# A gated graph network on one Trainium2 core: the first node tile's tanh stays in PSUM for its difference, its final sum goes to GpSimd, its low words are formed behind the loop

## The reference, cut to what matters

```python
def _gate(h, q, Wg, bg, Wq, bq):
    B, L, F = q.shape                      # 8, 64, 768
    h3 = h.reshape(B, N, F)                # N = 32 nodes for each of 8 graphs
    hg = jnp.einsum('bnf,gf->bng', h3, Wg[:, :F])
    qg = jnp.einsum('blf,gf->blg', q, Wg[:, F:]) + bg
    attn = jax.nn.sigmoid(hg[:, :, None, :] + qg[:, None, :, :])
    qi = jnp.einsum('bnlf,blf->bnf', attn, q)
    alpha = jax.nn.sigmoid(jnp.einsum('bnf,gf->bng', h3, Wq[:, :F]) + jnp.einsum('bnf,gf->bng', qi, Wq[:, F:]) + bq)
    hn = alpha * jnp.tanh(qi) + (1.0 - alpha) * h3
    return hn.reshape(B * N, F)

h = jax.nn.relu(_rgcn(x, W_rel1, W_root1, b1, src, dst, edge_type))
h = _gate(h, query_embs, Wg, bg, Wq, bq)
h = jax.nn.relu(_rgcn(h, W_rel2, W_root2, b2, src, dst, edge_type))
h = _gate(h, query_embs, Wg, bg, Wq, bq)
```

## Time and profile before

| what | us |
|---|---|
| median of 3 runs (lowest to highest) | 878.64 (878.55 to 879.24) |
| the profiled execution | 879.18 |
| its span in the profile | 877.4 |

### The profile page before, as it was taken

The page is one execution under the profiler, slowest core; times in us unless marked ns, Lnnn a source line. Parts: engine busy times, 40 slices in busy tenths (PEclk is TensorE's granted clock), DMA queues, the critical chain, the costliest instruction groups (busy, mean ns, idle before and its releaser), DMA issues.

```text
span 877.4 us, 10143 instructions
## 1 busy us (share of the span) xinstructions
PE 803.3 (92%) x4034; PEld 632.5 (72%) x4034; DVE 604.2 (69%) x671; ACT 388.4 (44%) x448; POOL 502.6 (57%) x214
## 2 busy tenths in 40 slices
PE   8999999999788999988997879999999998987987
PEld 3569976775455798666655459987997897864674
DVE  8955149999997622988999968534853888254451
ACT  1124366777663333766765524432342342241521
POOL 0346629999884472899998917661873478000000
PEclk9999999999999999999999989999999999979999
DMA  9036516254332452440533237633652653600000
GB/s 368 2 87 237 160 54 183 61 151 137 108 108 72 164 169 102 133 106 1 204 112 105 72 120 279 212 109 134 226 180 72 247 189 105 237 14 1 1 1 36
DMA packets 24262, 110.98 MB, mean 126 GB/s; under 512 B 3604, under 2 KB 5908, under 8 KB 23832
## 3 DMA queue, kind: packets, MB, share of 16 engines
q1 hardware_dynamic: 23096, 104.24, 36.3%
q10 hardware_dynamic: 1120, 6.10, 1.8%
HBM read 100.63 MB, written 0.79 MB: 116 GB/s over the span
## 4 chain that ended last, share of the span: by engine, by line
PE 61%; DVE 21%; POOL 12%; ACT 4%; issue 2%; DMA 0%; ACTq 0%; DVEq 0%
PE ps L958 22%; DVE prod L1679 12%; PE ps L906 11%; PE ps L943 6%; POOL prod L544 6%; POOL w_lo L532 4%; PE ps L1335 3%; DVE qi_t L1697 3%; PE ps L1195 2%; PE ps L1017 2%; POOL prod L547 2%; PE ps L1038 2%; PE ps L1148 2%; PE ps L1394 2%; PE ps L1320 1%
## 5 line engine op out<-in xcount | busy, mean ns | idle before, releaser
L532 POOL TENSOR_TENSOR w_lo<-w_raw,w_hi 128x1536 fp32r<-128x1536 f32 x54 | 201.5, 3742 | 148.6 <-ACT w_hi L598 148.5
L544 POOL TENSOR_TENSOR prod<-prod 128x1024 f32<-128x1024 f32 x94 | 223.5, 2400 | 49.1 <-DVE prod L1679 48.7
L705 ACT ACTIVATE prod<-ps 128x1024 f32<-128x1024 f32 x192 | 187.1, 1024 | 78.4 <-PE ps L1148 60.5
L1679 DVE TENSOR_TENSOR prod<-prod,ps 128x2048 f32<-128x2048 f32 x96 | 217.6, 2278 | 5.0 <-ACT prod L705 4.0
L1148 PE MATMUL ps<-sel_pair,h_and_q 128*128 128x512 f32 x384 | 129.7, 450 | 24.6 <-ACT prod L705 24.3
L906 PE MATMUL ps<-w_raw,h_t 128*128 128x384 f32 x408 | 141.7, 494 | 0.0
L598 ACT ACTIVATE w_hi<-w_raw 128x1536 fp32r<-128x1536 f32 x54 | 80.3, 1488 | 136.7 <-PE ps L958 92.9
L958 PE MATMUL ps<-w_hi,yt_hi 128*128 128x384 f32 x432 | 111.6, 339 | 8.1 <-POOL w_lo L532 8.1
L906 PEld LDWEIGHTS ps<-w_raw,h_t 128*128 128x128 f32 x408 | 78.7, 194 | 46.6 <-issue 2.6
L1148 PEld LDWEIGHTS ps<-sel_pair,h_and_q 128*128 128x128 f32 x384 | 67.2, 191 | 60.6 <-ACT prod L705 40.4
L958 PE MATMUL ps<-w_lo,yt_hi 128*128 128x384 f32 x432 | 110.4, 336 | 0.0
(11 more groups left out here) (189 smaller groups left out, 1001.8 us busy)
## 6 DMA issues: line engine op xcount, KB each, us to landing
w_raw<-weights SPq DMA_DIRECT2D x105, 768.0 KB, 4.4
wa_in<-weights SPq DMA_DIRECT2D x6, 768.0 KB, 5.8
w_gat<-weights SPq DMA_DIRECT2D x6, 768.0 KB, 8.0
w_query<-weights SPq DMA_DIRECT2D x3, 768.0 KB, 11.2
h_and_q<-stage_hi SPq DMA_DIRECT2D x24, 96.0 KB, 2.1
h_and_q<-stage_lo SPq DMA_DIRECT2D x24, 96.0 KB, 2.2
a_vec<-gat_vectors ACTq DMA_DIRECT2D x1, 2048.0 KB, 8.2
q_t<-queries ACTq DMA_DIRECT2D x1, 1536.0 KB, 10.6
```

Of the source, the lines that this page charges most:

```text
L532: pool.tensor_tensor(Wl[:, j, :], raw_slab(U, 0, j), Wh[:, j, :], ALU.subtract).then_inc(w_lo_ready, 1)
L544: pool.tensor_tensor(v[:, :, 0:32], v[:, :, 0:32], v[:, :, 32:64], ALU.add).then_inc(folded_once, 1)
L705: act.activation(slot_view(s)[:, :, 32 * u:32 * u + 32], args.rearrange("p b (n l) -> p (b n) l", l=LH), ACT.Sigmoid).then_inc(sigmoid_rea ...
L1679: TT(slot_view(s), slot_view(s), ps[:, 6, o:o + L].unsqueeze(1).broadcast_to([P, NB, L]), ALU.mult).then_inc(products_ready, 1)
```

## The change

The tanh of the first tile stays in PSUM bank 7, written over its own input. `gate_diff` is cut into two parts of 512 and 256 columns that read it there, at steps 29 and 32, and TensorE's next use of the bank waits for the difference, not for the tanh. `gate_add` leaves VectorE and stands in GpSimd's queue behind the fold of step 34. `h_lo` of the first tile leaves steps 38 and 43 and stands behind the loop, between `last_diff` and `last_half`.

```diff
 # GpSimd
+            def gate_add(i):
+                pool.wait_ge(alpha_diff_ready, 3 * i + 1)
+                if i == 0:
+                    pool.tensor_tensor(H[:, 0, :], H[:, 0, :], tq[:], ALU.add).then_inc(h_ready[0], 1)
+                else:
+                    pool.wait_ge(state_added, 1)
+                    pool.tensor_tensor(X[:, 0, :], X[:, 0, :], tq[:], ALU.add).then_inc(gate_x_ready, 1)
...
                 for s in range(STEPS - 1):
                     fold(i, s)
+                    if s == 34:
+                        gate_add(i)
                     if i == 1 and s == 38:
                         rstd(1, 0)
 # ScalarE
                 def gate_tanh(part):
                     act.wait_ge(qi_turned, 4 * i + (part + 1))
-                    c0, c1 = ((0, 512), (512, F))[part]
-                    act.activation(tq[:, c0:c1], ps[:, 7, 0:c1 - c0], ACT.Tanh).then_inc(tanh_ready, 1)
+                    n = (512, F - 512)[part]
+                    act.activation(ps[:, 7, 0:n], ps[:, 7, 0:n], ACT.Tanh).then_inc(tanh_ready, 1)
 # TensorE, bank7_free
                     if kind == "q":
-                        pe.wait_ge(tanh_ready, 4 * i + (m + 1))
+                        pe.wait_ge(diff_ready, 4 * i + (m + 1))
 # VectorE
-                def gate_diff():
-                    dve.wait_ge(tanh_ready, 4 * i + 2)
-                    TT(tq[:], tq[:], H[:, 0, :], ALU.subtract).then_inc(diff_ready, 1)
+                def gate_diff(part):
+                    c0, c1 = ((0, 512), (512, F))[part]
+                    dve.wait_ge(tanh_ready, 4 * i + part + 1)
+                    TT(tq[:, c0:c1], ps[:, 7, 0:c1 - c0], H[:, 0, c0:c1], ALU.subtract).then_inc(diff_ready, 1)
                 def gate_scale():
-                    dve.wait_ge(diff_ready, 3 * i + 1)
+                    dve.wait_ge(diff_ready, 4 * i + 2)
                     dve.wait_ge(alpha_ready, 3 * i + 1)
                     TT(tq[:], tq[:], alpha[:], ALU.mult).then_inc(alpha_diff_ready, 1)
-                def gate_add():
-                    dve.wait_ge(alpha_diff_ready, 3 * i + 1)
-                    if i == 0:
-                        TT(H[:, 0, :], H[:, 0, :], tq[:], ALU.add).then_inc(h_ready[0], 1)
-                    else:
-                        dve.wait_ge(state_added, 1)
-                        TT(X[:, 0, :], X[:, 0, :], tq[:], ALU.add).then_inc(gate_x_ready, 1)
...
                     if h == 0:
-                        dve.wait_ge(diff_ready, 3 * i + 3)
+                        dve.wait_ge(diff_ready, 4 * i + 4)
...
-                    if s == 33:
-                        gate_diff()
+                    if s in (29, 32):
+                        gate_diff((s - 29) // 3)
                     if s == 34:
                         gate_scale()
-                    if s == 35:
-                        gate_add()
-                    if i == 0 and s == 38:
-                        h_lo(1, 0)
                     if i == 1 and s == 36:
                         dve.wait_ge(gate_x_ready, 1)
                         norm_stats(1, 0)
                     if i == 1 and s == 40:
                         norm_shift(1, 0)
-                    if i == 1 and s == 43:
-                        h_lo(2, 0)
                 reduce(STEPS - 1)
                 reduce(STEPS - 2)
                 for part in range(2):
                     last_diff(part)
+                h_lo(i + 1, 0)
                 for h in range(2):
                     last_half(h)
```

## The result

The changed kernel takes 867.12 us (median of 4 runs, 866.25 to 868.16) against 878.94 (878.55 to 880.63): ratio 0.9866, 95% interval 0.9847 to 0.9885. That is 11.8 us less where 8.4 were forecast. Its profiled execution took 866.25 us, with a span of 864.4 against 877.4: 13.0 less.

The account below looks back on a forecast made before the run. VectorE was taken to set the time, with little air on GpSimd. Gains of 4.6 us in round one and 3.8 in round two make 8.4: from 879.18 profiled to 870.8, or 870.2 as median; range 866.0 to 874.5.

Parts of the forecast that it names:

- The sum over the loops: Both gate rounds: 4.6 us less in round one and 3.8 in round two, together 8.4.
- The difference from PSUM: VectorE, steps 29 and 32: 0.92 us without a wait, gaining 2.2 in round one and 1.75 in round two.
- `gate_scale` was to wait 1.0 more: VectorE, either round: waits 1.0 us more, for GpSimd's second fold of step 33; bounds 0 and 2.4.
- The sum on GpSimd: `gate_add` behind step 34's fold: 1.85 us on GpSimd, bounds 1.35 and 2.40; VectorE gains 2.4 a round.
- Rival (a): GpSimd's queue binds from step 34 in both rounds, adding 1.85 us a round: 873.9 us; chance 0.18.
- The give-back in round one: VectorE waits for GpSimd's second folds, about 0.5 us at step 36 and 1.0 at 39; 1.6 given back.
- `norm_shift` was to lose 0.8: Round two: meets an earlier-starting fold of step 39, 1.7 us instead of 0.88; bounds 0.7 gained, 1.5 lost.
- The low words: First tile's `h_lo` leaves the loops, gaining 2.6 and 1.4 us; its 0.96 behind them fits idle time, costing nothing.
- The added wait of TensorE: Step 32: TensorE turns the second query part only after the first difference; margin 1.4 us in round two, cost nothing.
- rival (d): Slower: a late first difference holds TensorE's turn and all behind it; 880.2 us if 10 late, 884 if 12; chance 0.07.
- The clock: TensorE's clock in round one's tail: a shorter wait could return up to 1 us; nothing taken.
- Rival (b): GpSimd keeps up and nothing collides, so the gain is 12.8 us: 865.8 us; chance 0.15.

Follow-up runs that it names:

- the filling: The kernel before, with 11 products without result on TensorE ahead of round one's last query products; 877.09 us against 879.03, ratio 0.9984.
- step 39: The changed kernel, with round one's step 39 folded on TensorE instead of a second time on GpSimd; 869.87 us, ratio 0.9901.
- sigmoid and step 39: The changed kernel, with the first tile's sigmoid left in PSUM and round one's step 39 folded on TensorE; 867.97 us, ratio 0.9876.
- GpSimd twice: The changed kernel, with a useless 128x768 product on GpSimd ahead of the sum in both rounds; 869.88 us, ratio 0.9899.
- the last kernel above: The changed kernel, with the first tile's sigmoid left in PSUM and products without result in TensorE's waits behind both loops; 865.33 us, ratio 0.9839.

## Why the prediction was right

**The sum over the loops** was 4.6 + 3.8 = 8.4; it is 4.05 + 4.62 = 8.67. Its terms:

- The difference from PSUM was put at 0.92 and is 0.93 net (0.60 + 0.33), with no wait, in both rounds.
- `gate_scale` was to wait 1.0 more; it takes 1.92 in both rounds against 0.95 before: 0.97. The run with the sigmoid in PSUM shows that it is the wait.
- The sum on GpSimd was put at 1.85 and is 1.82. Rival (a), that GpSimd pays it in full in both rounds, is out: putting it back on VectorE costs 0.5 and 2.5 us in the loops. Its mechanism holds in round one alone, up to step 39, where one more instruction on GpSimd comes out whole on the loop.
- The give-back in round one was put at 1.6, all of it waits for second folds. These waits, at steps 36 and 39, are 0.15 and 0.70 (0.5 and 1.0 forecast). The sentence that failed is "After 39 the steps are once-folded or folded on TensorE, and GpSimd falls behind no more": GpSimd folds five times on end up to 262.22, and TensorE's own fold stands behind it. TensorE's and VectorE's timelines after:

```profile
255.39 2.60 PE L1206 MATMUL ps<-prod,ident 128*128 128x128 f32 x16 [2.14 <-POOL prod L544]
```
```profile
250.65 0.69 DVE L1708 TENSOR_REDUCE qi_t<-prod 128x32 f32<-128x512 f32 x1 [0.70 <-POOL prod L547]
...
260.85 2.29 DVE L1690 TENSOR_TENSOR prod<-prod,ps 128x2048 f32<-128x2048 f32 x1 [0.47 <-ACT prod L716]
...
263.70 2.29 DVE L1690 TENSOR_TENSOR prod<-prod,ps 128x2048 f32<-128x2048 f32 x1 [0.56 <-ACT prod L716]
```

  The fold of step 41 waits 2.14 us, the arguments behind it come late, and VectorE waits 0.47 and 0.56 for sigmoids: 1.03 in which the forecast saw no wait. The wait for GpSimd alone does not cost this; TensorE's clock, 0.65 there, does, as the kernel with the same wait and a clock of 1.00 shows. In all 1.88 were given back, 0.85 to GpSimd and 1.03 to the clock.
- `norm_shift` was to lose 0.8; it takes 0.91 against 0.88. GpSimd's fold of step 39 was to start earlier relative to it. It does not: it starts 1.41 us ahead of it (466.28 and 467.69), 1.44 in the kernel before (477.55 and 478.99), and in both `norm_shift` ends with that fold. This term was 0.8 too low.
- The low words cost nothing behind the loop: 0.95 us, with 0.18 of the idle time left.
- The added wait of TensorE (rival (d)) cost nothing: the first difference of round two ends at 433.01, and no wait of TensorE for it stands on the chain of either round.

So the sum came nearer than its rounds: round one gave 4.05 where 4.6 were forecast, round two 4.62 where it was 3.8, and the two errors cancel. That part is luck.

**The clock** is the term that was mis-sized. I took nothing and allowed 1 us, in the stretch behind round one alone. The two stretches there gave 1.65 + 1.51 = 3.2, the one ahead of step 29 gave 0.97, and loop one lost 1.03. That this is TensorE's clock is shown by the granted shares (0.84 to 1.00 over the same work behind round one), by the filling, which brings the first of them about in the old kernel, and by the two kernels with the same wait at the fold of step 41 and different clocks. What remains of the 13.0, 1.07 - 0.79 and the small terms, lies in stretches with no edit that vary as much among the other kernels. The median moved by 11.8. Rival (b) was near in time (865.8) but not in cause: both the waits and the collisions were there.

## What to carry to other kernels

A VectorE instruction with two inputs in SBUF, beside a GpSimd that is hardly ever idle, costs its own time and the rest of GpSimd's running instruction; leaving one input in PSUM halves it, and GpSimd's next instruction gets its time back too. When work goes to an engine with little air, walk its queue to the end of the loop, through every engine that takes from it (here TensorE's folds), not only to the first consumer. And a gain of a few microseconds in a loop can be doubled or given back by TensorE's clock, in the stretch behind it or in the loop itself, so read the granted clock of every stretch and cut both traces at the same events before putting a cause to the whole.

## What was not expected of the hardware

- TensorE's clock in the stretch behind round one's loop is full or falls, and the wait ahead of it does not decide that alone. After waits of 2.70 and 2.71 us (low words alone, before, sum on VectorE) and of 2.16 and 2.17 (sum on GpSimd alone, step 39, sigmoid and step 39) it fell; after 1.42, 1.46 and 1.76 (GpSimd twice, after, sigmoid in PSUM) it stayed; but it also stayed after one of 2.73 us (difference from PSUM alone):

```profile
269.30:278.32 9.02, 9.02 (x33) 5.74 (x34) 7.58 (x7) 0.98 (x2) 3.77 (x3) 1.00 0.01 2
```

  What else decides is open. Inside loop one it is the same: with a wait of 2.13 us ahead of the same fold the clock fell in the last kernel above and stayed with the sigmoid in PSUM.
- GpSimd's 128x768 product of a tile with itself takes 1.49 us, the sum of two different tiles 1.84, in the same place of the same kernel. Whether one tile or the product makes it shorter, no run separates.
